# First attention: key-major score matmuls of four heads as 32-row tiles, two heads at a time

## The reference

```python
xq  = ada_ln(x_q,  t_vec, Wss_q,  bss_q)
xkv = ada_ln(x_kv, t_vec, Wss_kv, bss_kv)
q = (xq @ Wq + bq).reshape(B, Lq, 16, 16)
k, v = split(xkv @ Wkv + bkv)
scores = einsum('bqhd,bkhd->bhqk', q, k) / sqrt(16)
out = einsum('bhqk,bkhd->bqhd', softmax(scores), v).reshape(B, Lq, 256)
x = x_q + (out @ Wp + bp)
```

## Time and profile before

| | |
|---|---|
| median of 3 runs | 501.45 us |
| lowest and highest of the runs | 498.39 and 504.14 us |
| span of the profiled execution | 497.4 us |
| TensorE busy in it | 456.4 us, 92% |
| VectorE, ScalarE, GpSimd busy | 326.9, 183.0, 152.1 us |
| granted TensorE clock, mean | 0.986 of 2.4 GHz |

### The profile page before, as it was taken

How to read it: one execution, slowest core, us unless ns; L and a number is a source line. 1 busy time by engine, 2 the same in 40 slices (tenths; PEclk the granted TensorE clock), 3 DMA queues, 4 the chain that set the end, 5 groups by cost and what they waited for, 6 DMA issues and landing times.

```text
span 497.4 us, 6873 instructions
## 1 busy us (share of the span) xinstructions
PE 456.4 (92%) x2418; PEld 357.0 (72%) x2418; DVE 326.9 (66%) x794; ACT 183.0 (37%) x323; POOL 152.1 (31%) x211
## 2 busy tenths in 40 slices
PE   2657999999999999999977999999999999999994
PEld 2545665776676666766456888888888898888883
DVE  6878757376746754755877448875697657842445
ACT  1260434343344534335442254423444334532210
POOL 9347037204400400100005323354233533315333
PEclk9997999999999999999999899999999999999998
DMA  8701001610020011000011000001000010001001
GB/s 293 310 1 33 10 1 43 234 43 1 21 65 1 1 42 44 0 1 1 1 38 32 0 2 0 2 1 43 1 0 1 3 42 1 1 2 42 1 1 42
DMA packets 7314, 17.45 MB, mean 35 GB/s; under 512 B 880, under 2 KB 2288, under 8 KB 7152
## 3 DMA queue, kind: packets, MB, share of 16 engines
q1 hardware_dynamic: 5040, 11.57, 6.5%
q10 hardware_dynamic: 1584, 3.15, 1.7%
q0 software_dynamic: 656, 2.29, 1.7%
HBM read 14.45 MB, written 2.10 MB: 33 GB/s over the span
## 4 chain that ended last, share of the span: by engine, by line
PE 81%; DVE 11%; issue 3%; POOL 2%; ACT 2%; DMA 1%; POOLq 0%; DVEq 0%
PE bank L1110 52%; PE pair L1110 14%; PE pair L1203 4%; PE bank L1245 3%; PE bank L1242 3%; DVE lnt L783 2%; DVE nm L894 1%; PE bank L1211 1%; PE bank L1255 1%; DVE rs L767 1%; DVE keys L855 1%; DMA ctx_sb<-in_ctx 1%; DVE st L757 1%; PE bank L1266 1%; POOL rs L542 1%
## 5 line engine op out<-in xcount | busy, mean ns | idle before, releaser
L579 POOL TENSOR_TENSOR hs<-hid,hs 128x512 fp32r<-128x512 f32 x48 | 64.2, 1338 | 125.9 <-DVE hs L1063 125.9
L1110 PE MATMUL bank<-nx,w1h 128*128 128x512 f32 x224 | 74.0, 412 | 0.0
L1110 PE MATMUL pair<-w2h,hs 128*128 128x256 f32 x384 | 70.5, 282 | 0.0
L728 ACT ACTIVATE hid<-bank,ab 128x512 f32<-128x512 f32 x48 | 33.0, 689 | 89.6 <-PE bank L1110 89.5
L1110 PEld LDWEIGHTS pair<-w2h,hs 128*128 128x128 f32 x384 | 62.7, 190 | 4.4 <-POOL hs L579 0.2
L894 DVE TENSOR_REDUCE nm<-pair 128x4 fp32r<-128x616 f32 x64 | 51.1, 798 | 19.7 <-PE pair L1203 19.1
L1063 DVE CAST hs<-hid 128x512 fp32r<-128x512 f32 x48 | 20.6, 430 | 57.9 <-ACT hid L728 57.1
L657 ACT ACTIVATE pt<-bank 128x512 f32<-128x512 f32 x80 | 47.2, 598 | 28.6 <-PE bank L1110 26.0
L1110 PE MATMUL pair<-w2l,hs 128*128 128x256 f32 x192 | 54.2, 282 | 0.0
L1110 PE MATMUL bank<-wh,m_ev 128*128 128x512 f32 x112 | 44.5, 398 | 0.0
L1110 PE MATMUL bank<-nx,w1l 128*128 128x512 f32 x112 | 44.4, 396 | 0.0
(11 more groups left out here) (190 smaller groups left out, 921.2 us busy)
## 6 DMA issues: line engine op xcount, KB each, us to landing
stage<-in_w1n POOLq DMA_DIRECT2D x7, 256.0 KB, 3.2
w1e_sb<-in_w1e SPq DMA_DIRECT2D x1, 1792.0 KB, 7.9
x_sb<-in_x SPq DMA_DIRECT2D x3, 512.0 KB, 14.5
stage<-in_w1a SPq DMA_DIRECT2D x3, 512.0 KB, 6.7
stage<-in_ew2T SPq DMA_DIRECT2D x3, 512.0 KB, 3.9
out_x<-x_sb SPq DMA_DIRECT2D x3, 512.0 KB, 2.7
wss_sb<-in_wss SPq DMA_DIRECT2D x2, 512.0 KB, 8.7
x_sb<-in_x ACTq DMA_DIRECT2D x1, 512.0 KB, 4.9
```

Source lines behind the costliest of these rows:

```text
L579: g_.tensor_tensor(hs[:, q % 3, 1, :], hid[:, q % 2, :], hs[:, q % 3, 0, :], ALU.subtract).then_inc(hl_r, 1)
L728: A(dst, B_H[n % 2][:, :], ACT.Silu, bias=ab1[:, m, c // CPB:c // CPB + 1]).then_inc(h_r, 1)
L1110: ins = mm(dst, a, b_, start=first and i == 0, stop=last and i == len(terms) - 1, skip_group_check=free)
```

## The change

The four main heads of `keys` become two steps of two heads each: `("keys", g, 0)` makes heads 0 and 2, `("keys", g, 1)` heads 1 and 3. Their matmuls take only the 32 rows of a head, heads k and k+2 lie in different row strips and go to different banks, and the four matmuls are issued as ka, ka, kb, kb. A second `keys` waits until both exponentials of the first are done. The tail becomes a step of its own, `tails`, with full-array matmuls as before. `rows` (the row maxima) keep full-array matmuls. The steps are written in another order around `fill[0]` and `fill[1]`.

```diff
-                order = [("keys", g, 0), more and ("rows", n, 0), ("keys", g, 1), fill[0], ("keys", g, 2),
-                         more and ("rows", n, 1), ("keys", g, 3), fill[1], ("keys", g, 4), more and ("rows", n, 2), fill[2]]
+                order = [("keys", g, 0), more and ("rows", n, 0), fill[0], more and ("rows", n, 1), ("keys", g, 1), fill[1],
+                         more and ("rows", n, 2), ("tails", g), fill[2]]
...
 # ScalarE
-            def keys(g, k):
-                n = (GH + 1) * g + k
-                act.wait_ge(st_d, n + 1)
...
-                A(pt[:, k, :], B_ST[n % 2][:, :], ACT.Exp, scale=DH ** -0.5).then_inc(ex_d, 1)
+            def keys(g, p):
+                for i in range(2):
+                    n = (GH + 1) * g + 2 * p + i
+                    act.wait_ge(st_d, n + 1)
...
+                    A(pt[:, p + 2 * i, :], B_ST[i][:, :], ACT.Exp, scale=DH ** -0.5).then_inc(ex_d, 1)
+
+            def tails(g):
+                act.wait_ge(st_d, (GH + 1) * (g + 1))
+                A(pt[:, GH, :], B_ST[0][:, :], ACT.Exp, scale=DH ** -0.5).then_inc(ex_d, 1)
...
 # TensorE
-            def keys(g, k):
+            def keys(g, p):
...
-                n = (GH + 1) * g + k
+                n = (GH + 1) * g + 2 * p
...
-                if n >= 2:
-                    pe.wait_ge(ex_d, n - 1)
-                if k < GH:
-                    a, b_ = ka[:, b, gi, LK * k:LK * k + P], kb[:, b, gi, P * k:P * k + P]
                 else:
-                    a, b_ = ka[:, b, gi, LK * GH:LK * GH + P], kb[:, b, gi, P * GH:P * GH + P]
-                passes(B_ST[n % 2][:, :], [(a, qh[:, g % 2, :]), (b_, ql[:, g % 2, :])]).then_inc(st_d, 1)
+                    pe.wait_ge(ex_d, n)
+                for i in range(2):
+                    k = p + 2 * i
+                    r = slice(32 * k, 32 * k + 32)
+                    mm(B_ST[i][:, :], ka[r, b, gi, LK * k:LK * k + P], qh[r, g % 2, :], start=True, stop=False)
+                for i in range(2):
+                    k = p + 2 * i
+                    r = slice(32 * k, 32 * k + 32)
+                    mm(B_ST[i][:, :], kb[r, b, gi, P * k:P * k + P], ql[r, g % 2, :], start=False, stop=True).then_inc(st_d, 1)
+
+            def tails(g):
+                c, gi = divmod(g, NG)
+                b = c // CPB
+                pe.wait_ge(ex_d, (GH + 1) * g + 3)
+                passes(B_ST[0][:, :], [(ka[:, b, gi, LK * GH:LK * GH + P], qh[:, g % 2, :]),
+                                       (kb[:, b, gi, P * GH:P * GH + P], ql[:, g % 2, :])]).then_inc(st_d, 1)
...
-                for j in range(GH):
-                    pe.wait_ge(ex_d, (GH + 1) * g + j + 1)
+                for n, j in enumerate((0, 2, 1, 3)):
+                    pe.wait_ge(ex_d, (GH + 1) * g + n + 1)
```

More of the change, by code:

```diff
@@ L648, in proj @@
                 A(qh[:, g % 2, :], B_P[g % 2][:, :], ACT.Identity, bias=sm("bq", g % NG)).then_inc(qh_r, 1)
-            def keys(g, k):
-                n = (GH + 1) * g + k
-                act.wait_ge(st_d, n + 1)
[L653 to L656, removed]
-                A(pt[:, k, :], B_ST[n % 2][:, :], ACT.Exp, scale=DH ** -0.5).then_inc(ex_d, 1)
+            def keys(g, p):
+                for i in range(2):
+                    n = (GH + 1) * g + 2 * p + i
+                    act.wait_ge(st_d, n + 1)
+                    if p == 0 and i == 0 and g:
+                        act.wait_ge(av_d, g)
+                    if n == 0:
+                        act.wait_ge(v_r, 2 * B)
+                    A(pt[:, p + 2 * i, :], B_ST[i][:, :], ACT.Exp, scale=DH ** -0.5).then_inc(ex_d, 1)
+            def tails(g):
+                act.wait_ge(st_d, (GH + 1) * (g + 1))
+                A(pt[:, GH, :], B_ST[0][:, :], ACT.Exp, scale=DH ** -0.5).then_inc(ex_d, 1)
             def av(g):
@@ L736, in _ @@
             first = {"m_taken": mpiece, "nxf": nxf_, "exp": exp, "wsplit": wsplit, "router": router}
-            walk(l0_steps(), {"xt": xt, "proj": proj, "keys": keys, "av": av, "zt": ztr, **first})
+            walk(l0_steps(), {"xt": xt, "proj": proj, "keys": keys, "tails": tails, "av": av, "zt": ztr, **first})
             walk(between_steps(), {"zt": ztr, **first})
@@ L1213, in shift @@
                 ins.then_inc(nm_d, 1)
-            def keys(g, k):
+            def keys(g, p):
                 c, gi = divmod(g, NG)
                 b = c // CPB
-                n = (GH + 1) * g + k
-                if k == 0:
+                n = (GH + 1) * g + 2 * p
+                if p == 0:
                     pe.wait_ge(ql_r, g + 1)
@@ L1418, in _ @@
             front_parts = {"nxt": nxt, "score": score, "wtr": wtr}
-            walk(l0_steps(), {"xt": xt, "val": val, "proj": proj, "rows": rows, "shift": shift, "keys": keys, "av": av, "prep": prep,
+            walk(l0_steps(), {"xt": xt, "val": val, "proj": proj, "rows": rows, "shift": shift, "keys": keys, "tails": tails, "av": av, "prep": prep,
                               **rows_parts, **front_parts})
```

## The result

The changed kernel takes 518.19 us in the median (516.95 to 523.50, 4 runs) and the kernel before, run beside it, 499.92 (497.59 to 504.14, 4 runs). The ratio is 1.038, with a 95% interval from 1.034 to 1.042: slower by 3.8%. I had forecast 510.6 with a range up to 518.0. The direction was right; the loss is twice the forecast one.

The account below looks back on a forecast made before the run. TensorE was taken to set the time on the whole (busy 456.4 of 497.4 us). Added waits by groups, 4.2 + 1.7 + 0.8 + 0.8 + 1.6 = 9.1 us, on the median 501.45 gave 510.6, range 501 to 518.

Parts of the forecast that it names:

- The walk: Group 8, first `keys` to `wp`: waits for maxima and the `zt` copy put `wp` at 5.21, for 4.16; 1.05 us longer.
- my sum: First attention, all groups: 4.2 + 1.7 + 0.8 + 0.8 + 1.6 = 9.1 us longer.
- The covered groups: Groups 0, 1, 2, 3, 6, 7, 11, 15: wait for maxima held or covered by other work; 0.2 us each, 1.6 in all.
- The column tiles of the earlier trace: Tiles of `av`, seen running four together, taken as stand-in for row tiles: 0.14 us going in, 0.19 coming out.
- The price of a visit: Switching into and out of tiles at each pair of `keys` heads: 0.33 us, making a pair 0.79 for 0.92.
- my rivals: Four alternatives: saving paid out, 0.12; switches nearly free, 0.15; row tiles not together, 0.1; delays taken up, 0.13.
- tiles that don't run together: Rival 3, pairs of `keys` heads: row tiles run one after the other, a pair takes 1.25 us; 519.6 us, chance 0.1.
- the signs that I named: Trace after: pair's matmuls two by two, next full-array 0.8 us behind, TensorE idle before second and third `rows` and `wp`, `wp` at 5.2.
- the rival: Rival 1, first `keys` to `wp`: TensorE's saving is paid out, distance 4.2 or less; 497.3 us, or 486.7 with free switches; chance 0.12.

## Why the prediction was right and wrong

**Right: what the order does.** The walk said that TensorE's saving would not be paid out, because the second `rows` must wait for the maxima, the second pair comes behind it, and ScalarE's copy of `zt` behind its exponentials. The trace shows each of these steps, and the order alone costs 9.0 us in the walk; my sum was 9.1. That the two are so near is in part luck, for the sum was made for tiled pairs and the 9.0 is of full-array ones. In the changed kernel itself, by the prediction's own terms, the ten distances without low clock should have grown by 5.6 us and grew by 5.1; the five with low clock should have grown by 3.3 and grew by 11.1. In group 8 I had 1.05 us and the trace has 0.68. Of the 0.37 between them 0.27 is the copy, which follows the exponentials' start by 0.97 (161.96 less 160.99) and not by 1.24; the exponentials follow their pair 0.08 sooner than predicted, and the second pair starts at 2.65 instead of 2.69. From one `av` to the next, groups 4 to 5 and 8 to 9 lost 0.66 and 0.69 (0.86 predicted), those ending in groups 12 and 13 lost 0.93 and 0.83 (1.05). The covered groups were near the 0.2 that I took: 0.27, 0.30, 0.30, 0.20 for those ending in 1, 6, 11 and 15.

**Right: that row tiles run together.** The column tiles of the earlier trace rows were a fair stand-in. The price of a visit was near too: 0.33 was taken and 0.4 measured around a single head. The prediction put the whole of it behind a pair's first matmul, where 0.79 was expected and 0.67 came; the other half lies ahead of it. From the start of `rows` a tiled pair takes 1.12 us, and two heads at the durations of the earlier trace rows take 1.20, so the saving is 0.08 a pair where 0.13 was predicted.

**Wrong: a missing term.** The step that failed is the one that made the sum: "On TensorE alone the change saves 0.13 a pair, 32 pairs, 4 us", with all other TensorE rows kept at their durations of before. They were not kept. TensorE went to the lower level of its clock in four stretches of the walk, and the five distances that hold them came out 7.6 us longer in the profiled run, measured against the same order without tiles; with it, and 0.5 less in the ten other distances, the 9.0 become the 16.1 measured in the walk. None of my rivals had it, and the upper end of the range had another cause, tiles that don't run together, which did not happen.

**What makes the clock fall.** That it comes with the tiles and not with the waits is shown: the same order with full-array matmuls keeps 0.985 with 6.6 us of the same waits, and the old order with tiles has 0.931 with none of them. A profile is one run, but all runs agree: the changed kernel had 0.941 to 0.960, the one without tiles 0.972 to 0.985. That the rows in use matter is shown by two pairs of kernels whose matmuls are the same in number, order and length, with 32 and with 64 rows: 0.941 to 0.954 against 0.970 to 0.981, and 0.950 to 0.958 against 0.970 to 0.979 over their runs. Single heads with the unused half of the array filled beside them point the same way, 0.934 to 0.950 without and 0.965 to 0.977 with, though there the number of matmuls grew as well. Against it stand single heads with 32 and 64 rows, which can't be told apart. Visits by themselves did little when the full-array work stayed, 0.973 to 0.980. Waits are not wholly without effect: the two other kernels with pairs and no tiles each had one short low stretch, at 142 to 146 and 78 to 82. What stays open is why 64 rows helped little in the changed kernel's own order (0.960 to 0.964), where the same 64 rows with the second pair earlier had no low stretch. A likely reason, not shown, is that waits and shorter matmuls count together with the rows; no run here changes one of these alone around the fall at 143 us.

**Of the signs that I named,** first `keys` to `wp` came out at 4.84 (named: 5.2, against 4.2 for the rival), the next full-array matmul 0.67 behind a pair's first (0.8), and TensorE idle ahead of the second `rows` and ahead of `wp`. It was not idle ahead of the third `rows` in group 8 (it was, by 0.32 us, in group 14).

No version beat the kernel before. The best, 64-row pairs with the second pair earlier, is 1.1% slower.

## What to carry to other kernels

Making an engine's work shorter pays only if the work that is released by it can start earlier too: here the second pair had to stand behind a `rows` that one bank and VectorE's 0.8 us hold back, so about 0.1 us saved per pair bought 0.6 to 0.9 us of waiting in such a group. Before cutting matmuls to the rows that carry data, ask what the array's clock does: in these runs rows of zeros were worth 8 to 9 us in two orders of steps, 4 in a third and nothing measurable one head at a time, and the granted clock by stretches is the view to read first. Half of the price of a visit to tiles stood ahead of the first tile matmul here: measure from the start of the full-array matmul before it to the start of the one behind. When a whole stage is longer by more than its waits, compare the distance of two equal instructions before and after.

## What was not expected of the hardware

- TensorE's granted clock can depend on how many rows of the array the matmuls use, at equal number and length: 0.953 and 0.981 for 32 and 64 rows in pairs, 0.958 and 0.979 in another order. It was 0.960 and 0.964 in a third, and 0.931 and 0.940, within the scatter of the runs, one head at a time; 0.970 there with the other 64 rows in use beside the head.
- One 32-row head and two side by side take the same, 0.66 and 0.67 us, and issuing ka, kb, ka, kb instead of ka, ka, kb, kb changes neither this nor the order in the trace: both ka start at 161.48, though a kb was written between them, so the start of tile matmuls does not keep the written order.
- A visit to 32-row tiles costs 0.4 us between full-array matmuls, around a head (1.14 for 0.74 us from the start of `rows`) and in the middle of a pair (1.30 for 0.93), half of it ahead of the first tile matmul in the first case.
- Two exponentials of 512 columns whose inputs are both ready take 1.08 to 1.09 us together, at 0.60 each alone.
